# Bias rows of a four-stage residual kernel: added by ScalarE and VectorE instead of by products

## The reference, cut to what matters

```python
# x: (B=8, S=1024, D=512) f32; each stage adds to x
x = x + zX*lap_x(x) + zY*lap_y(x) + zR*x*(1 - x)        # diffusion, scalars per batch
a = tanh(x @ W1 + b1); scores = a @ v                    # W1 (512,128)
x = x + (softmax(mask(scores)) @ x) / count              # mask: prefix, postfix or cloze, by token
x = x + x @ W[subject].T + b[subject]                    # W 512x512, by token of the batch
z = relu(x @ Wd[profile] + bd[profile])                  # 512 -> 128
y = x + z @ Wu[profile] + bu[profile]                    # 128 -> 512
x = x + (y - mean(y)) * rsqrt(var(y) + eps) * g[profile] + b3[profile]
```

## Time and profile before

| what | value |
|---|---|
| median of 3 runs | 586.56 us (584.38 to 588.13) |
| profiled execution | 590.16 us, its span 588.3 us |
| granted TensorE clock, mean | 0.974 |
| steady period on PE | 66.0 us, six of them |
| opening and `first`, up to the first period | 122.2 us |
| HBM read, written | 61.26 MB, 31.98 MB |

### The profile page before, as it was taken

The page is one execution under the profiler, slowest core; times in us unless marked ns, Lnnn a source line. Parts: engine busy times, 40 slices in busy tenths (PEclk is TensorE's granted clock), DMA queues, the critical chain, the costliest instruction groups (busy, mean ns, idle before and its releaser), DMA issues.

```text
span 588.3 us, 9302 instructions
## 1 busy us (share of the span) xinstructions
PE 554.8 (94%) x2928; PEld 439.8 (75%) x2928; DVE 432.9 (74%) x1163; ACT 337.3 (57%) x593; POOL 317.0 (54%) x276
## 2 busy tenths in 40 slices
PE   5997479999999999999999999999999999999995
PEld 2357466788869887788869887788869887788784
DVE  4654786779866996779866996779866996767356
ACT  3534357465855677465855677465855677455540
POOL 7014661388706983388706983388706983137321
PEclk8898769999999999999999999999999999999998
DMA  6148406795499748995499748995499748124252
GB/s 222 32 143 247 78 19 195 247 212 102 125 273 230 158 90 187 311 215 99 123 291 222 147 91 180 323 212 103 122 291 225 142 89 193 24 72 87 54 100 101
DMA packets 60000, 93.84 MB, mean 159 GB/s; under 512 B 10999, under 2 KB 15607, under 8 KB 59952
## 3 DMA queue, kind: packets, MB, share of 16 engines
q0 software_dynamic: 16544, 29.90, 33.5%
q1 hardware_dynamic: 33584, 46.53, 23.4%
q10 hardware_dynamic: 9824, 16.83, 7.6%
HBM read 61.26 MB, written 31.98 MB: 158 GB/s over the span
## 4 chain that ended last, share of the span: by engine, by line
PE 86%; DMA 4%; DVE 4%; ACT 2%; issue 2%; SPq 1%; ACTq 0%; POOL 0%; DVEq 0%
PE y L633 37%; PE front_ps L760 9%; PE front_ps L679 8%; PE front_ps L633 8%; PE front_ps L702 4%; PE front_ps L647 3%; PE front_ps L724 3%; PE y L816 3%; PE front_ps L687 2%; PE front_ps L693 2%; DMA xn<-in_x 2%; PE y L661 1%; DMA xu<-in_x 1%; DMA tok_i<-in_itok_B 1%; PE front_ps L734 1%
## 5 line engine op out<-in xcount | busy, mean ns | idle before, releaser
L530 POOL TENSOR_TENSOR norm<-norm 128x1 f32<-128x1 f32 x64 | 52.9, 833 | 145.9 <-DVE norm L1600 145.9
L633 PE MATMUL y<-wth,x2h 128*128 128x512 f32 x256 | 102.6, 401 | 0.0
L633 PE MATMUL y<-wth,x2l 128*128 128x512 f32 x256 | 100.6, 393 | 0.0
L633 PE MATMUL y<-wtl,x2h 128*128 128x512 f32 x256 | 100.1, 391 | 0.0
L543 POOL TENSOR_TENSOR x2l<-x2f,x2h 128x1024 fp32r<-128x1024 f32 x32 | 79.3, 2480 | 24.3 <-ACT x2h L957 23.8
L511 POOL TENSOR_TENSOR xd<-xn 128x1024 f32<-128x1024 f32 x28 | 85.1, 3438 | 12.0 <-DVE x L1443 12.0
L537 POOL DMA_DIRECT2D out<-o_sb x58 | 57.5, 1095 | 45.3 <-ACT o_sb L1112 43.1
L1589 DVE BATCH_NORM_STATS2 stats<-y 128x6 f32<-128x512 f32 x64 | 44.4, 693 | 48.6 <-PE y L633 48.6
L760 PE MATMUL front_ps<-th_pt,x 128*128 128x129 f32 x512 | 68.1, 284 | 6.4 <-DVE x2f L1573 6.3
L1573 DVE SCALAR_TENSOR_TENSOR x2f<-alb,small,front_ps 128x128 f32<-128x128 f32 x256 | 71.2, 339 | 3.1 <-issue 1.9
L760 PEld LDWEIGHTS front_ps<-th_pt,x 128*128 128x128 f32 x512 | 65.9, 198 | 10.1 <-DVE x2f L1573 7.7
(11 more groups left out here) (155 smaller groups left out, 1150.4 us busy)
## 6 DMA issues: line engine op xcount, KB each, us to landing
xn<-in_x SPq DMA_DIRECT2D x32, 512.0 KB, 11.2
out<-x ACTq DMA_DIRECT2D x58, 256.0 KB, 4.5
out<-o_sb POOLq DMA_DIRECT2D x58, 256.0 KB, 5.0
xu<-in_x SPq DMA_DIRECT2D x21, 512.0 KB, 10.6
xu<-in_x POOLq DMA_DIRECT2D x21, 512.0 KB, 7.6
wn<-in_L_cond_weight SPq DMA_DIRECT2D x8, 1024.0 KB, 5.3
wd<-in_L_cond_down_w SPq DMA_DIRECT2D x8, 256.0 KB, 5.4
wu<-in_L_cond_up_w SPq DMA_DIRECT2D x8, 256.0 KB, 2.6
```

The lines of the kernel that those rows point to most:

```text
L530: pool.tensor_tensor(rstd[:, r:r + 1], ve[:, r:r + 1], minus_half[:, :], ALU.pow).then_inc(rstd_ready, 1)
L633: ins = mm(dst, lhs, rhs, start=first and q == 0, stop=last and q == len(parts) - 1, skip_group_check=True)
```

## The change

- The products with `rows_on` go, and with them `rows`, `bias`, `bias_all`, `spread_bias`, `keep_bias`, `round_bias`. Three rows per batch are broadcast by DMA to all partitions: linear bias (`start_row`), last bias (`rest_row`), up bias (`up_row`). POOL adds the up bias to `start_row` (`start_sum`) and subtracts it from `rest_row` (`rest_difference`).
- ACT seeds the bank of every tile with `start_row`; DVE's new `keep_x3` adds `rest_row` while it copies the bank to `x3`.
- The three banks are one ring over the batches, `bank(b, t) = ys[(8b + t) % 3]`.
- The scalars go to one partition and are spread by a product with ones; two products `keep_warm` stand in front of it. The mask is copied by a DMA of SP from the three prepared ones, by token (`load_mask`), and `take_mask` goes. `add_identity` is one instruction. `ends_f` is built on narrow views.
- SP's loads of x are split into `load_above` and `load_own`, and SP has an order of its own in the frame.
- All engines have new orders. Beside those below: ACT's `opening` has `seed_rows` ahead of `square`; POOL's `first` begins with `rest_difference(0)`, `add_below(1, 0)`, `add_below(1, 1)`; DVE's `steady` has `keep_x3(b, 2)` to `keep_x3(b, 7)`, `keep_x3(n, 0)` and `keep_x3(n, 1)` spread among the rest, with `subtract_mean(b, 7)` ahead of the diffusion of chunks 2 and 3 and `add_identity(m)`, `rest_z(n, 1)`, `mask_scores(m, 0)`, `mask_scores(m, 1)` at the end. `adapter_down(0, 0)` stands ahead of the weight's transposes in PE's `first`.

```diff
-        wn = sb("wn", [P, KD, D])
+        wn_wd = sb("wn_wd", [P, KD + 1, D])
+        wn = wn_wd[:, 0:KD, :]
+        wd = wn_wd[:, KD, :].rearrange("p (k a) -> p k a", a=P)
+        w_diagonal = wn_wd[:, :, :].rearrange("p k h -> p (k h)").rearrange("p (k h) -> p k h", h=D + P)[:, :, 0:P]
         wth = sb("wth", [P, KD, D], F32R)
         wtl = sb("wtl", [P, KD, D], F32R)
-        wd = sb("wd", [P, KD, P])
...
-        rows = sb("rows", [P, D])
-
-        bias = sb("bias", [P, 2, D], F32R)
         g_row = sb("g_row", [P, 2, D])
-        bias_all = sb("bias_all", [P, D])
+        start_row = sb("start_row", [P, 2, D])
+        rest_row = sb("rest_row", [P, 2, D])
+        up_row = sb("up_row", [P, D])
...
-            def load_x(n, c):
+            def load_above(n, c):
 
                 r0, size = c * 2 * P, 2 * P
-
-                wait_past(sp, l0_done, NC * (n - 1) + c + 1)
+                if n > 1:
+                    sp.wait_ge(l0_done, NC * (n - 1) + c + 1)
...
+            def load_own(n, c):
+
+                r0 = c * 2 * P
+                sp.wait_ge(l0_done, NC * (n - 1) + c + 1)
+                sp.dma_start(xn[:, c, :, 1:D + 1], x[bass.ds(n, 1), r0:r0 + 2 * P, :].rearrange(
+                    "b (j p) d -> p (b j) d", p=P)).then_inc(x_loaded[c], 16)
 
...
+                def fetch(dst, a, token_value):
+                    sp.dma_start(dst, a[bass.ds(token_value, 1), :].to_broadcast([P, D])).then_inc(row_loaded, 16)
+
+                wait_past(sp, start_ready, n)
+                wait_past(sp, rest_ready, n)
+                fetch(up_row[:, :], L3_ub, profile)
+                wait_past(sp, y_seeded, NJ * (n - 1))
+                fetch(start_row[:, n % 2, :], L2_b, subject)
+                wait_past(sp, x3_ready, NJ * (n - 1))
+                fetch(rest_row[:, n % 2, :], L3_b, profile)
...
-            def load_scale(n, q):
+            def load_scale(n):
                 profile = token(itok_B_0_6, n, NPROF)
 
-                wait_past(sp, y_free, NJ * (n - 1) + CREDIT)
-                sp.dma_start(g_row[:, q, :], L3_g[bass.ds(profile, 1), :].to_broadcast([P, D])
-                             ).then_inc(g_loaded, 16)
-
-            def load(n, q):
-
-                load_rows(n)
-                load_linear(n)
-                load_scale(n, q)
-                for c in range(NC):
-                    load_x(n + 1, c)
-
-            for c in range(NC):
-                load_first(c)
-            load_constants()
-            load_linear(0)
-            load_rows(0)
-            load_scale(0, 0)
-            for c in range(NC):
-                load_x(1, c)
-            for n in range(1, B - 1):
-                load(n, n % 2)
-            load_rows(B - 1)
-            load_linear(B - 1)
-            load_scale(B - 1, 1)
+                wait_past(sp, y_free, NJ * (n - 1))
+                sp.dma_start(g_row[:, n % 2, :], L3_g[bass.ds(profile, 1), :].to_broadcast([P, D])
+                             ).then_inc(g_loaded[n % 2], 16)
+
+            def load_mask(n):
+                kind = token(itok_B_0_2, n, 3)
+
+                sp.wait_ge(const_made, 2)
+                wait_past(sp, al_ready, n)
+                sp.dma_start(mask[:, :], masks[:, bass.ds(kind, 1), :].rearrange("p o m -> p (o m)")
+                             ).then_inc(mask_loaded, 16)
+
+            def load_next(m, c):
+
+                if m + 1 < B:
+                    load_above(m + 1, c)
+                    load_own(m + 1, c)
+
...
+            def first():
+
+                load_rows(1)
+                load_scale(1)
+                load_next(1, 0)
+                load_mask(1)
+                load_linear(1)
+                load_next(1, 1)
+                load_next(1, 2)
+                load_next(1, 3)
+
+            def steady(b, n, m, q):
+
+                if m is not None:
+                    load_rows(m)
+                    load_scale(m)
+                    load_next(m, 0)
+                    load_mask(m)
+                    load_linear(m)
+                    load_next(m, 1)
+                    load_next(m, 2)
+                    load_next(m, 3)
+
...
-            def rest_up_and_bias(n, q):
-
-                pool.wait_ge(wuh_ready, n + 1)
-                pool.tensor_tensor(wul[:, q, :], wu[:, :], wuh[:, q, :].bitcast(F32),
-                                   ALU.subtract).then_inc(wul_ready, 1)
-                pool.wait_ge(wul_ready, n + 1)
-                pool.wait_ge(bias_h, n + 1)
-                rest = bias[P // 2:P, q, :]
-                pool.tensor_tensor(rest, rows[P // 2:P, :], rest.bitcast(F32),
-                                   ALU.subtract).then_inc(bias_ready, 1)
-                pool.wait_ge(bias_ready, n + 1)
+            def start_sum(n):
+
+                pool.wait_ge(row_loaded, 48 * n + 48)
+                row = start_row[:, n % 2, :]
+                pool.tensor_tensor(row, row, up_row[:, :], ALU.add).then_inc(start_ready, 1)
+
+            def rest_difference(n):
+
+                pool.wait_ge(row_loaded, 48 * n + 48)
+                row = rest_row[:, n % 2, :]
+                pool.tensor_tensor(row, row, up_row[:, :], ALU.subtract).then_inc(rest_ready, 1)
...
+            def spread_scalars():
+
+                pe.wait_ge(scalars_in, 16 * SCALAR_DMAS)
+                pe.wait_ge(ones_made, 1)
+                mm(scalars, ones[0:1, :], raw3[0:1, :, :].rearrange("p q b -> p (q b)"), start=True, stop=True
+                   ).then_inc(scalars_ps, 1)
...
-                if t < 2 or t == 7:
-                    pe.wait_ge(y_free, NJ * b + before(t, YB) + 1 + CREDIT)
-                    mm(y[:, :], rows_on[:, 0, :], bias[:, q, :], start=True, stop=False, skip_group_check=True)
-                elif t == 2:
-                    pe.wait_ge(bias_kept, b + 1)
-                else:
-                    pe.wait_ge(y_seeded, len(SEEDED) * b + SEEDED.index(t) + 1)
+                y = bank(b, t)
+                pe.wait_ge(y_seeded, NJ * b + t + 1)
...
-                mm(y[:, :], rows_on[:, 1, :], bias[:, q, :], start=False, stop=False, skip_group_check=True)
...
-            def keep_bias(n):
-                act.wait_ge(bias_ps, n + 1)
-                copy(bias_all[:, :], ys[2][:, :]).then_inc(bias_kept, 1)
-
             def seed(b, t):
 
-                act.wait_ge(y_free, NJ * b + before(t, YB) + 1 + CREDIT)
-                copy(ys[t % YB][:, :], bias_all[:, :]).then_inc(y_seeded, 1)
-
-            def keep_x3(b, t):
-                act.wait_ge(y_ps, NJ * b + t + 1)
-
-                act.wait_ge(base_stored[t % XB], 16 * (NJ // XB * b + t // XB) + 16)
-                copy(x3[:, t % XB, :], ys[t % YB][:, :]).then_inc(x3_ready, 1)
+                act.wait_ge(start_ready, b + 1)
+                if NJ * b + t < YB:
+                    act.wait_ge(rows_taken, NJ)
+                else:
+                    act.wait_ge(y_free, NJ * b + t - YB + 1)
+                copy(bank(b, t)[:, :], start_row[:, b % 2, :]).then_inc(y_seeded, 1)
...
-                diagonal = wn[:, :, :].rearrange("p k h -> p (k h)")
-                for k in range(KD):
-                    d = diagonal[:, k * (D + P):k * (D + P) + P]
-                    ins = dve.tensor_tensor(d, d, ident[:, :], ALU.add)
-                ins.then_inc(wn_ready, 1)
+                ident_all = ident[:, :].rearrange("p (o h) -> p o h", o=1).to_broadcast([P, KD, P])
+                dve.tensor_tensor(w_diagonal, w_diagonal, ident_all, ALU.add).then_inc(wn_ready, 1)
...
+            def keep_x3(b, t):
+
+                dve.wait_ge(rest_ready, b + 1)
+                dve.wait_ge(y_ps, NJ * b + t + 1)
+                if b == LAST and t - XB >= FIRST_LAST:
+                    dve.wait_ge(last_sum, t - XB - FIRST_LAST + 1)
+                else:
+                    dve.wait_ge(base_stored[t % XB], 16 * (NJ // XB * b + t // XB) + 16)
+                dve.tensor_tensor(x3[:, t % XB, :], bank(b, t)[:, :], rest_row[:, b % 2, :],
+                                  ALU.add).then_inc(x3_ready, 1)
...
@@ vector, first() @@
                 maxima(0)
                 block_weights(0)
+                adapter_bias(0)
                 row_weights(0)
                 rest_v(0)
                 probabilities(0, 0)
-                adapter_bias(0)
+                add_around(1, 0)
                 probabilities(0, 1)
+                times_x(1, 0)
+                add_around(1, 1)
+                diffuse(1, 1, 0)
                 carry_products(0, 0)
                 carry_sums(0, 0)
...
@@ tensor, steady() @@
 
+                transpose_p(n, 1)
                 transpose_alpha(n)
-                transpose_p(n, 1)
-                pool_blocks(n, q, 0, (0,))
                 adapter_up(b, 1 - q, 3)
                 pool_blocks(n, q, 0, (1,))
+                pool_blocks(n, q, 0, (0,))
                 pool_blocks(n, q, 0, (2,))
-                linear(b, 1 - q, 4)
                 pool_blocks(n, q, 1, (0, 1))
```

(78 more changed lines are left out.)

452 lines of the change are left out of this document (194 added, 258 removed).

## The result

The changed kernel took 617.79 us (median of 4 runs, 615.29 to 620.62), the one before 587.35 (4 runs, 584.38 to 591.27): ratio 1.0515, 95% interval 1.0436 to 1.0595, slower. The forecast was 584.0 with a range of 553 to 598; the result lies outside. The profiled execution took 617.02 around a span of 615.2.

A forecast was written before the change was run, and what follows sets the result against it. PE's own work was taken to bound the six periods. Opening 109.5, periods 403.2, clock 6.8 and tail 66.2 summed to a span of 585.7, less 1.7 to the median: 584.0 us, range 553 to 598.

The forecast's parts named there:

- term 3: SP's queue: next weights wait behind `subtract_mean(b, 7)`, x and three tokens; PE stands about 4.4 us, period 67.6.
- Term 1: PE: 96 bias-row products removed at 0.23 each; a PE-bound period takes about 63.2, 17 us over six.
- rival 1: Weights not late, PE stays the bound at 63.2 per period: 553 us; chance 0.24.
- Term 2: DVE takes `keep_x3`, +4.9 per period: busy about 55.5 of 63, packed but not the bound.
- landing 4.9 behind that (4.8 to 6.4): Step of term 3: time from the last of the four weight loads' issue to its landing.
- Behind `block_sums`: Stretch on PE from `block_sums` to its next entry into `steady`, claimed to take 8.8 us.
- Term 4: PE's clock halves after the idle, costing up to 1.7 us each, taken in four of six periods: +6.8.
- Term 5: Opening and `first`: PE's first entry into `steady` at 109.5 us, -12.7 (bounds -4 to -19).
- Term 6: The tail behind the six periods: 18 products fewer, 4.1 less 0.5, giving 66.2 us.
- Rival 2: Same loads later still: +2.4 for tokens, +1.5 for landing, 598 us; chance 0.18 shared with an opening without gain.
- the bound of 72 for a period: Upper end of term 3's bounds, 64.5 to 72 us, around its period of 67.6.

The follow-up runs named there:

- e1: Changed kernel, with SP issuing the next batch's weight loads right behind `load_rows`, ahead of `load_scale`: 560.41 us, ratio 0.9535 to the kernel before.
- e10: The e1 kernel with 12 products per batch added back, 96 in all, as many as the change removed: 582.02 us.
- e8: Changed kernel, with POOL's last two accumulating stores of a batch waiting until the weights have landed (not in the last two batches): 601.76 us.
- e7: Changed kernel with nine more unused float32 products per period on PE before `block_sums`, to fill its idle: 625.17 us.
- e2: Changed kernel, with three token registers (mask and weights) read ahead of the wait for `y_free`, order of transfers kept: 577.81 us.
- e9: Changed kernel with both edits, those of e4 and e8: median 590.76 us over 10 runs, 573.22 to 597.39.
- e11: The e9 kernel, with POOL's `left_and_right` waiting until DVE's identity add is done: 570.18 us, ratio 0.9687 to the kernel before.
- e5: The kernel before, with only SP's weight loads moved behind the scale row and first chunk of x: 608.05 us, ratio 1.0329.
- e4: Changed kernel, with DVE's `add_identity` moved behind the maxima and `keep_x3` of tile 2, no longer ahead of the mask scores: 590.81 us.

## Why the prediction was wrong

The mechanism was term 3's, to the instruction; its size was not. By the same cuts as the prediction:

- **Term 1, right.** 12 products per period at 0.23: periods of 63.2 to 65.0 in e1, 66.8 with the products back (e10). e1's 560.4 is rival 1's case, forecast at 553. One of its periods is 1.8 longer, where `keep_x3` waits 2.28 for a store of its slot, and one 1.6 longer, by the `pn` of which the part behind `block_sums` tells.
- **Term 2, right in the main.** `keep_x3` has a mean of 0.68, and `subtract_mean(b, 7)` ends 35.0 behind T0 in the second period, forecast 34.5.
- **Term 3, failed in one number.** SP issued `bd_col` 12.4 us behind that, forecast 12.5; the three tokens between `xn` and `wn` took 7.5, forecast 7.5. There luck helped: none took the 2.5 that I gave to each, but the first 3.9, right behind the loads of x, and the other two 1.8. From the landing to `block_sums` 6.2, forecast 6.3. Between them stands the step that failed, "landing 4.9 behind that (4.8 to 6.4)": it was 9.2. I had taken the duration of a transfer from a place in the period where POOL's queue moved 144 packets, 0.26 MB, from 221 to 230 us (55 of them, 0.11 MB, by 228.7, when the weights had landed), and moved it to a place with 288 packets, 0.52 MB, without asking what POOL and ACT issue there. The kernel before had a warning: in its last two periods, where POOL moved 0.3 MB beside the weights, the landing took 6.2 and 6.4. e8 shows the stores as the cause of 3.3 of the 4.3; the rest was not taken apart.
- **Behind `block_sums`, mis-sized.** From `block_sums` to the next T0 11.3 us instead of 8.8. Of the 2.5, the half clock makes about 1.0 (e7). The rest stands at the full clock too: to the transposes of alpha e2 needs 10.65, e1 9.0 in four of its first five periods and 10.5 in the other. The 1.5 between them goes with the eight small `pn` of DVE (`probabilities`). They take 2.18 in the four, and 4.45 to 4.47 in the other and in all five of e2. In the long one of e1 two of the eight take 1.42 and 1.56 instead of 0.34:

```profile
361.05 1.42 DVE L1500 SCALAR_TENSOR_TENSOR pn<-pn,small,ident 128x128 f32<-128x128 f32 x1
...
362.65 1.56 DVE L1500 SCALAR_TENSOR_TENSOR pn<-pn,small,ident 128x128 f32<-128x128 f32 x1
362.79 4.41 POOL L563 TENSOR_TENSOR start_row<-start_row,up_row 128x512 f32<-128x512 f32 x1
```

The first of them is over before POOL's 128x512 sum begins, when the rows of POOL hold only DMA issues. So that sum can't be the whole cause, and whether this is the block of e9 stays open.

- **Term 4, right in its sum.** Forecast 6.8; about 1.0 in five periods, 5. It came in all five with the long idle, not in four of six (the sixth, with an idle of 1.6, kept the full clock), and each cost less than the 1.7 I took, as another wait was hidden under it.
- **Term 5, right.** First T0 at 106.8, forecast 109.5; `pool_blocks` starts at 50.02, forecast 50, and the idles of 5.7 and 5.3 are gone. **Term 6:** 67.65, forecast 66.2.

The ledger: 585.7 was forecast as span, 615.2 measured. The opening gives -2.7, the tail +1.5, the periods +30.8 (440.8 against 403.2 and the 6.8 of term 4). Of these, the later arrival of the weights is some 5.1 in each of five (4.5 the landing, 9.4 on average there; the rest mostly the longer first period), 25.5; the path behind `block_sums` 2.5 in each, 12.5, less the 6.8 forecast as term 4: together 31.2. The sixth period came as forecast. Rival 2 had the right direction at the wrong place: it gave the landing 6.4 at most and put the rest on the tokens, which were as forecast. The range ended at 598 because its prices came from the kernel before, where the weights never met more than those 0.3 MB of stores. It was too narrow by the prediction's own figures as well: the 2.4 and 1.5 of rival 2 are 3.9 a period and 23 in six, of which it took 14, and the bound of 72 for a period would have given 610. The five slow periods measured 75.1 on average, beyond that bound too.

## What to carry to other kernels

When a load is moved, its landing is not moved with it: look up what the other queues have in flight at the new place (here two accumulating stores), and price it by a row that has the same company. On an in-order engine ask of every wait which instructions behind it need nothing of what it waits for; here moving one add of 0.69 us was worth some 27 us. Put loads that a period needs ahead of those that only the next one needs, and register loads ahead of the wait that would otherwise be followed by them.

## What the runs showed of the hardware

- **An add on DVE stood still until POOL was done.** An add of two SBUF operands on DVE that takes 0.69 alone took 3.07 when a 128x1024 sum on POOL had started 0.03 us before it, and ended 0.57 behind POOL's end (e9). In all five periods of e9 in which they met, the add ended 0.55 to 0.57 behind POOL's; a wait that keeps them apart makes it 0.68 (e11). The Trainium skill (SBUF — State Buffer, SBUF: two separate sides) says that the two share a pair of ports as a lock held for a whole instruction, and that a DVE operation with two SBUF inputs needs it when POOL's reads SBUF. The trace agrees: the add ended about as if it had begun when POOL was done.
- **Stores of another queue held up loads in flight.** Two accumulating stores of POOL, 0.5 MB, held 25% of the engines' time, and the last of 1.3 MB of loads beside them landed in 9.2 instead of 5.9 us (changed kernel and e8).
- **The clock fell by no fixed length of idle that these runs show.** `down_through_w` ran at the full clock behind idles of 1.5 (e2), 1.6 (the sixth period of the changed kernel) and 2.5 (e7), and slowed behind 0.95 and 1.4 (e5), 1.8 and 2.7 (both e7), 3.6 (e4) and 8.3 (the changed kernel). The shortest, in e5:

```profile
179.44 5.35 PE L703 MATMUL front_ps<-wd,wn 128*128 128x128 f32 x32 [0.95 <-DVE wn L1457]
```

What decides between 0.95 and 2.5 stays open.
